# Scores in three bursts of 4, 3 and 3 instead of four, values together, maxima turned at full width, and the transform's sums on GpSimd

## The reference, cut to what matters

```python
q = (x @ wq).reshape(bsz, seq_len, N_HEADS, HEAD_DIM)      # k, v alike, 8 heads; rotary on q and k
scores = jnp.einsum('bqhd,bkhd->bhqk', q, k) / np.float32(np.sqrt(HEAD_DIM)) + mask
attn = jax.nn.softmax(scores.astype(jnp.float32), axis=-1)
out = jnp.einsum('bhqk,bkhd->bqhd', attn, v).reshape(bsz, seq_len, N_HEADS * HEAD_DIM)
return out @ wo
# experts: relu(x W_e + b_e) of the top 2 of 8, averaged; g = silu of it; x = x + s * g
# second layer's kernel: sums over 64 states of v / (g(omega) - Lambda), four of them, 512 roots
cauchy = lambda v: (v[None, :] / denom).sum(-1)
at_roots = c * (k00 - k01 * (1.0 / (1.0 + k11)) * k10)
```

## Time and profile before

| | |
|---|---|
| Time, median of 3 runs | 664.26 us (659.87 to 670.34) |
| Span of the profiled execution | 663.2 us |
| Median less span: what lies around the span | 1.1 us |
| PE busy | 627.2 us, 95% |
| DVE busy | 552.0 us, 83% |
| ACT busy | 287.0 us, 43% |
| POOL busy | 238.2 us, 36% |

### The profile page before, as it was taken

One profiled execution on the slowest core, in us unless ns is written; L12 is line 12 of the kernel. 1 busy time (PEld: TensorE's weight loads), 2 busy tenths in 40 slices (PEclk: granted clock), 3 DMA queues, 4 the chain that ended last, 5 costly groups with the idle time before them and its releaser, 6 DMA issues.

```text
span 663.2 us, 12226 instructions
## 1 busy us (share of the span) xinstructions
PE 627.2 (95%) x3565; PEld 338.9 (51%) x3565; DVE 552.0 (83%) x1788; ACT 287.0 (43%) x535; POOL 238.2 (36%) x364
## 2 busy tenths in 40 slices
PE   8999999998999999999999999999999999789997
PEld 5788784433433334433443344443444343478886
DVE  6698999869978888989888798897789975689994
ACT  4353325434434435444444444443455443444441
POOL 3777641333323212332221322322222115576620
PEclk9999999969989999999999999999999999899999
DMA  7599989889788564675954649667276527768842
GB/s 262 141 336 266 337 239 173 146 164 273 152 268 161 166 139 80 154 132 188 194 105 98 136 109 220 125 173 152 52 167 111 171 72 241 156 145 217 217 104 79
DMA packets 79902, 113.10 MB, mean 171 GB/s; under 512 B 9704, under 2 KB 42664, under 8 KB 79840
## 3 DMA queue, kind: packets, MB, share of 16 engines
q1 hardware_dynamic: 68098, 86.90, 53.5%
q0 software_dynamic: 6704, 18.62, 11.8%
...
## 4 chain that ended last, share of the span: by engine, by line
PE 55%; DVE 25%; DMA 8%; issue 4%; SPq 3%; POOL 2%; ACT 1%; ACTq 0%; DVEq 0%; POOLq 0%
PE bank L1672 13%; DVE bank L1390 12%; PE bank L1023 8%; PE bank L1591 7%; PE bank L2162 6%; PE bank L1644 5%; PE bank L1683 4%; PE bank L2167 4%; DMA w_e<-expert_rows,slots 3%; PE bank L1617 3%; DVE arena L1390 2%; DMA qt<-arena 2%; DMA qt<-turned_parts 2%; DVE m_parts L1403 2%; DVE m_parts L1405 1%
## 5 line engine op out<-in xcount | busy, mean ns | idle before, releaser
L1390 DVE CUSTOM_DVE_ANT_0 bank<-bank,cst 128x384 f32<-128x384 f32 (+3 forms) x512 | 234.9, 521 | 47.6 <-PE bank L1591 44.5
L1514 ACT ACTIVATE arena<-bank 128x512 f32<-128x512 f32 x320 | 170.9, 599 | 180.2 <-PE bank L1617 149.7
L1332 POOL TENSOR_SCALAR_AFFINE_SELECT arena<-arena 128x512 f32<-128x512 f32 x128 | 80.7, 643 | 309.2 <-ACT arena L1514 309.2
L1672 PE MATMUL bank<-w_e,arena 128*128 x312 | 162.2, 626 | 0.0
L1591 PE MATMUL bank<-kt,qt 48*128 48x512 f32 (+1 forms) x496 | 111.0, 338 | 5.6 <-DVE arena L1390 5.0
L1591 PEld LDWEIGHTS bank<-kt,qt 48*128 48x128 f32 x496 | 70.1, 187 | 83.9 <-DVE arena L1390 51.7
L1617 PE MATMUL bank<-qt,kt 50*128 50x512 f32 x256 | 88.2, 452 | 2.4 <-DMA qt<-arena 2.0
L1644 PE MATMUL bank<-arena 128*32 128x512 f32 (+3 forms) x1024 | 84.8, 445 | 0.4 <-ACT arena L1514 0.4
L1672 PEld LDWEIGHTS bank<-w_e,arena 128*128 128x128 f32 x312 | 54.6, 193 | 58.0 <-issue 54.3
L1390 DVE DVE_READ_ACCUMULATOR2_ANT arena<- 128x1 f32 x512 | 71.9, 140 | 0.0
L1683 PE MATMUL bank<-w_proj,arena 128*128 128x512 f32 x128 | 67.6, 636 | 0.0
...
...
## 6 DMA issues: line engine op xcount, KB each, us to landing
...
```

What stands on the lines that cost most here:

```text
L1332: g.affine_select(out=diag, in_=diag, compare_op=ALU.is_ge, fill=0.0, base=0, pattern=[[0, 2], [0, HALF], [1, P]], channel_multiplier=-1). ...
L1390: i = v.tensor_tensor_reduce(out=part, in0=part, in1=const("mask")[:, S - w:], scale=1.0, scalar=LOWEST, op0=ALU.add, op1=ALU.max, accum_o ...
L1514: nc.scalar.activation(pt[:, s, first:second + 1:second - first].rearrange("p c r q -> p c (r q)"), s2_bank(b, h, n).rearrange("p (c x) -> ...
L1672: i = t.matmul(bank[7], xgt[:, m % 2, k * P:(k + 1) * P], w_e[:, ex[m], k, :], start=False, stop=(k == KB - 1))
```

## The change

Scores. The first scores of the following group and the second scores of the group go out in three bursts instead of four: S1(3 to 6) with S2(0 to 3), S1(7 to 9) with S2(4 to 6), and S1(0 to 2) of the group after with S2(7 to 9). All four blocks of values follow each other behind the third burst. `SIZES` has four gaps, with groups of 6, 8, 8 and 6 quarters; names for the first six, the eight and the last six are BACK, EIGHT and FRONT.

Maxima. They are copied unsplit into a wide tile (`maxima_columns`), turned as 128 columns into bank 4 instead of a bank of the first scores, and split after the turning by two operations over 128 x 128 (`maxima_rows`). The turning stands after at most three quarters of the second gap; `normalise` of the group before stands ahead of the split, `pair_rows` behind it.

Queues. SP issues its small transfer of the maxima before the stores of finished expert rows, not behind them. ACT issues its own after exponential 7, or before emptying the bank in groups with four quarters in the second gap.

Sums. Of the six steps of a piece the last four run on POOL (`pool_sums`), at the end of its list for the group, with the sum over 64 states made by halving.

```diff
@@ -45,11 +45,12 @@
 BLOCKS = [(j, t) for j in range(TPB) for t in range(j, TPB)]
 PAIRED = [((0, 0), (0, 1)), ((0, 2), (0, 3)), ((2, 2), (2, 3)), ((1, 1), (3, 3)), ((1, 2), (1, 3))]
 ORDER = [0, 2, 3, 1]
-GAPS = 5
+GAPS = 4
+TURN_AFTER = 3
 PLAN = "x" * 12 + ("ooxoo" + "x" * 9) * 2 + "ooxoo" + "x" * 6
-SIX, EIGHT = (2, 1, 1, 1, 1), (2, 2, 1, 1, 2)
+BACK, EIGHT, FRONT, SIX = (2, 2, 2, 0), (2, 4, 2, 0), (2, 3, 1, 0), (2, 2, 2, 0)
 NONE = (0,) * GAPS
-SIZES = [NONE, (0, 0, 0, 2, 2)] + [SIX, EIGHT] * 12 + [SIX, SIX] + [SIX, EIGHT, (2, 2, 1, 1, 0), NONE]
+SIZES = [NONE, (0, 0, 2, 2)] + [BACK, EIGHT, EIGHT, FRONT] * 6 + [SIX, SIX] + [BACK, EIGHT, FRONT, NONE]
 QUARTERS = [SIZES[KV * b:KV * (b + 1)] for b in range(NB)]
...
@@ -89,10 +90,10 @@
 
     first, last, at = times_of(0), times_of(KB - 1), {}
     for m in range(MT):
-        t = first[m] - 2 + m if m < 2 else max(first[m] - 2, last[m - 2])
-        t += -1 if t % 2 == 0 and (m < 2 or t > last[m - 2]) else t % 2 == 0
-        assert t < first[m]
-        at.setdefault((t // (4 * KV), t // 4 % KV, t % 4 // 2), []).append(m)
+        free = last[m - 2] if m > 1 else GAPS
+        slots = [t for t in range(free, first[m]) if t % GAPS in (1, 2)]
+        t = max([t for t in slots if t < first[m] - 1] or slots)
+        at.setdefault((t // (GAPS * KV), t // GAPS % KV, t % GAPS - 1), []).append(m)
     return at
...
@@ -693,20 +699,35 @@
                 e.wait_ge(dve_steps, st.count())
                 tt(den_r, den_r, den_a, ALU.mult)
                 tt(den_i, den_i, den_a, ALU.mult)
+
+        def pool_sums(e, st, b, h):
+
+            g = nc.gpsimd
+            piece, step = divmod(b * NG + h - 2, 6)
+            if piece not in range(NB) or step < 2:
+                return
+
+            def tt(out, a, b, op):
+                g.tensor_tensor(out, a, b, op).then_inc(pool_steps, st.one())
+                e.wait_ge(pool_steps, st.count())
+
             shape = [P, 4, NS]
             n_r, n_i = (num[:, c].rearrange("p l r n -> p (l r) n") for c in (0, 1))
             d_r, d_i = (d.unsqueeze(1).to_broadcast(shape) for d in (den_r, den_i))
-            for c, x, y, op in ((0, n_r, n_i, ALU.add), (1, n_i, n_r, ALU.subtract)):
-                if h == 2 + 2 * c:
-                    tt(big[0], x, d_r, ALU.mult)
-                    tt(big[1], y, d_i, ALU.mult)
-                if h == 3 + 2 * c:
-                    tt(big[2], big[0], big[1], op)
-                    v.tensor_reduce(part_sum[:, c], big[2], AX.X, ALU.add).then_inc(dve_steps, st.one())
-                    e.wait_ge(dve_steps, st.count())
-            if h == 5:
-                v.tensor_copy(sums[:, :, bass.ds(piece, 1), :], part_sum.unsqueeze(2)).then_inc(dve_steps, st.one())
-                e.wait_ge(dve_steps, st.count())
+            c = step // 2 - 1
+            x, y, op = ((n_r, n_i, ALU.add), (n_i, n_r, ALU.subtract))[c]
+            if step % 2 == 0:
+                e.wait_ge(s4_den, piece + 1)
+                alone(e)
+                tt(big[0], x, d_r, ALU.mult)
+                tt(big[1], y, d_i, ALU.mult)
+            else:
+                tt(big[2], big[0], big[1], op)
+                w = NS // 2
+                while w > 1:
+                    tt(big[2][:, :, 0:w], big[2][:, :, 0:w], big[2][:, :, w:2 * w], ALU.add)
+                    w //= 2
+                g.tensor_tensor(sums[:, c, piece].unsqueeze(2), big[2][:, :, 0:1], big[2][:, :, 1:2], ALU.add).then_inc(s4_sums, 1)
 
         def dve_roots(e, st, step):
...
@@ -1370,14 +1394,18 @@
         QUERIES_OF = ((3,), (3,), (2, 0), (2, 0), (1, 1))
         LOWEST = -3.0e38
 
-        def first_half(n):
-
-            return (n + 1) % 2, n // 2
+        def first_half(b, h, n):
+
+            return (n + (b * NG + h < 2)) % 2, n // 2
+
+        def turned_at(b, h):
+
+            return bank[(0, 1)[h] if b * NG + h < 2 else 4][:, 0:P]
 
         def maxima(e, b, h, n):
 
             v = nc.vector
-            s, kind = first_half(n)
+            s, kind = first_half(b, h, n)
             if n == 0 and due(at := nth_of(1, b, h, 0)):
                 e.wait_ge(b_mx, at)
             e.wait_ge(b_s1, nth_of(NJ, b, h, n + 1))
...
@@ -1392,25 +1420,22 @@
                 at += w
             i.then_inc(b_m, 1)
 
-        def maxima_parts(e, st, b, h):
+        def maxima_columns(e, b, h):
+
+            e.wait_ge(b_m, nth_of(NJ, b, h, NJ))
+            rows = row_max.rearrange("p (s r) t -> p s (r t)", s=2)
+            nc.vector.tensor_copy(m_cols[:, :, 0:2], rows.unsqueeze(2).to_broadcast([P, 2, 2, HALF * TPB])).then_inc(b_mx, 1)
+
+        def maxima_rows(e, st, b, h):
 
             v = nc.vector
-            e.wait_ge(b_m, nth_of(NJ, b, h, NJ))
-            if due(at := nth_of(1, b, h, 0)):
-                e.wait_ge(b_tm, at)
-            e.wait_ge(dve_steps, st.count())
-            rows = row_max.rearrange("p (s r) t -> p s (r t)", s=2)
-            v.tensor_scalar(m_parts[:, :, 0], rows, -1.0, None, ALU.mult).then_inc(dve_steps, st.one())
-            e.wait_ge(dve_steps, st.count())
-            v.scalar_tensor_tensor(out=m_parts[:, :, 1], in0=rows, scalar=-1.0, in1=m_parts[:, :, 0].bitcast(F32),
-                                   op0=ALU.mult, op1=ALU.subtract).then_inc(b_mx, 1)
-
-        def maxima_rows(e, b, h):
-
             e.wait_ge(b_tm, nth_of(1, b, h, 1))
             if due(at := nth_of(32, b, h, 0)):
                 e.wait_ge(b_mr, at)
-            nc.vector.tensor_copy(m_rows, S1_BANK[nth_of(NJ, b, h, NJ + 2) % 3][0:2 * 2 * HALF * TPB, 0:P]).then_inc(b_me, 1)
+            v.tensor_copy(m_high[:, :], turned_at(b, h)).then_inc(dve_steps, st.one())
+            e.wait_ge(dve_steps, st.count())
+            v.scalar_tensor_tensor(out=m_rows[:, :], in0=m_high[:, :].bitcast(F32), scalar=const("less"), in1=turned_at(b, h),
+                                   op0=ALU.mult, op1=ALU.add).then_inc(b_me, 1)
 
         def dve_b(e, st):
             v = nc.vector
...
@@ -1463,25 +1488,27 @@
                     following = next_group(b, h, 1) if b * NG + h + 1 < NB * NG else None
                     after = next_group(b, h, 2) if b * NG + h + 2 < NB * NG else None
                     if following:
-                        for n in (2, 3, 4):
+                        for n in (3, 4, 5, 6):
                             maxima(e, *following, n)
                     done, later = next_group(b, h, -1), h > 0 and following
                     rows_of(*done)
                     if not later:
                         divided(*done)
                     if following:
-                        for n in range(5, NJ):
+                        for n in (7, 8, 9):
                             maxima(e, *following, n)
-                        maxima_parts(e, st, *following)
+                        maxima_columns(e, *following)
+                    if later:
+                        normalise(*done)
+                    if following:
+                        maxima_rows(e, st, *following)
+                    if later and done[1] % 2:
+                        pair_rows(done[0], done[1] // 2)
                     for m in TURNS.get((b, h, 0), ()):
                         expert_x(m)
-                    if following:
-                        maxima_rows(e, *following)
                     if after:
-                        for n in (0, 1):
+                        for n in (0, 1, 2):
                             maxima(e, *after, n)
-                    if later:
-                        divided(*done)
                     if (b, h) == (NB - 1, NG - 1):
                         dve_tap_parts(e)
                         dve_scale(e)
...
@@ -1533,20 +1562,22 @@
 
             def go(b):
                 for h in range(1 if b == 0 else 0, NG):
-                    for n in (0, 1, 2):
+                    following = next_group(b, h, 1) if b * NG + h + 1 < NB * NG else None
+                    for n in (0, 1, 2, 3):
                         exps(e, b, h, n)
                     results(b, h, 0)
-                    for n in (3, 4, 5):
+                    for n in (4, 5, 6):
                         exps(e, b, h, n)
+                    early = len(WORK[b, h, 1]) > TURN_AFTER
+                    if following and early:
+                        maximum_rows(e, *following, 1)
                     results(b, h, 1)
-                    for n in (6, 7):
-                        exps(e, b, h, n)
-                    results(b, h, 2)
-                    if b * NG + h + 1 < NB * NG:
-                        maximum_rows(e, *next_group(b, h, 1), 1)
+                    exps(e, b, h, 7)
+                    if following and not early:
+                        maximum_rows(e, *following, 1)
                     for n in (8, 9):
                         exps(e, b, h, n)
-                    results(b, h, 3, 4)
+                    results(b, h, 2, 3)
 
             for b in range(NB):
                 go(b)
...
@@ -1569,15 +1600,15 @@
```

(35 more changed lines are left out.)

46 lines of the change are left out of this document (28 added, 18 removed).

## The result

The changed kernel takes 688.25 us (median of 4 runs, 685.90 to 690.95). The kernel before, run on the same chip, takes 665.40 (4 runs, 659.87 to 670.34). The ratio is 1.0335, with a 95% interval from 1.0299 to 1.0372: 3.3% slower, some 22 us, and outside the range of the prediction.

What follows compares the result with a forecast made beforehand. PE was taken to set the pace, DVE having little to spare. The order saves 12 us, late DVE adds 1.5 and waits for stacks 14: 3.5 slower than the median 664.3, about 667 us (range 660 to 676).

Steps and rivals of the forecast that it cites:

- new order with its DVE waits: PE's order over groups 2 to 30: some 12 us less, with 1.5 us more for late DVE in groups 2 and 3.
- PE idle for the stacks: PE waits for queries and keys before the third burst: six waits of 2.2 us and one of 0.6, 14 us more.
- The stacks arrive later: Prediction's section on SP's 12 loads of queries and keys: they land after PE needs them behind FRONT groups, 14 us more.
- I take 2.2: Assumed wait in us for stacks in each of six BACK groups, from a span of 1.2 to 3.0, or 3.7.
- The deadline: After FRONT, the BACK group's third burst needs the stacks at T+11.9 us, T being the start of the turning.
- The rule that I cited: 16 partitions reach 4 of 16 ports, 104 GB/s at 1 MiB; by it alone the 12 loads would take 11.3 us.
- The wait in the burst of four: Fourth score pair waits 0.63 us for DVE to read its bank; burst 1.78 us, 18 us over 29 groups.
- The timetable: PE's work by group: BACK 12.7, EIGHT 14.3, FRONT 12.0 us; four groups 53.2 against 54.9 before.
- the transform's sums cost nothing: Four of six sum steps moved from DVE to POOL: hidden in POOL's idle time, no wait of PE ends in them.
- The stacks in time: Rival: the 12 loads find emptier queues and land in time, 653 us; chance 0.18.
- No wait in the burst of four: Rival: that wait is absent or absorbed by the turning's own wait, 18 us less, 649 us; chance 0.10.
- The slower one: Rival: stores ahead of the loads weigh fully, FRONT costs 3.7 and first EIGHT 1.0 us, 682 us; chance 0.16.
- POOL's sums holding DVE up: Rival: GpSimd's sums delay DVE or a select in up to 16 groups, 10 us more, 677 us; chance 0.06.

Runs made afterwards that it cites:

- both kernels without loads: The 12 stack loads in groups of odd h left out of each kernel: changed kernel 653.06 us, kernel before 660.93 us.
- the waits filled: Changed kernel with 14 matmuls on constants into idle bank 7 before the first scores that wait for stacks, in six groups: 678.56 us.
- the experiment with alternating halves: Changed kernel with the 12 stack loads going to lower and upper half of the partitions in turn: 684.34 us.
- the fourth pair apart: Changed kernel with queries loaded in two parts, and the burst of four made three pairs, one quarter, the fourth pair, one quarter: 655.04 us.
- the split loads: Changed kernel with the second group's queries in six later transfers on their own semaphore: 659.92 us; the same on the kernel before: 665.35 us.
- the sums on DVE: Changed kernel with the four sum steps of each piece moved back from POOL to DVE: 688.18 us.

## Why the prediction was wrong

It said 667 us; it is 688.25. The order and its waits for DVE came out nearly as worked out, the price of the waits for the stacks did not. By the forecast's sum against what was measured:

| term | forecast | measured | by |
|---|---|---|---|
| new order with its DVE waits | -10.5 | -7.9 | both kernels without loads |
| PE idle for the stacks | +14 | +20.2 | waits of PE in the trace after |
| clock behind those waits | none | +9.7 | the waits filled |
| sum | +3.5 | +22.0 | 22.85 between the medians |

**The failed step is the price of the waits in "The stacks arrive later": "I take 2.2" for each of six, "14 us" in all.** It was too low twice: the loads were taken as too short, which is 6.2 us, and a wait was charged with its own length alone, so that the clock behind it stood in the sum at nothing, which is 9.7 us.

**The length of the loads.** The deadline was right: PE could begin S1(0) at 269.44, 11.67 after the turning of the FRONT group (forecast T+11.9). The issue came even sooner than forecast, at T+1.80 where no store stands ahead and T+2.24 with one (forecast T+2.43). But the loads took 12.4 to 13.5 us behind FRONT groups, 13.0 in the mean, so that PE waited 2.55 to 3.92, 3.11 in the mean of six. The 2.2 stands for loads of 11.7 us. I took that from 14 cases before and held it fixed, though the change moves the loads against POOL's gathers. Of the excess of 1.3 us, about 1.1 go with the gathers, by the experiment that moved them; the rest stays open.
The rule that I cited, the Trainium skill's "SBUF — State Buffer", section "Door 1: The DMA port swizzle", gave 11.3 us for these loads, and I wrote that the trace agrees. The kernel after does not agree: 13.0, for the same bytes to the same partitions. The measurement decides, and the experiment with alternating halves found no gain by other ports.

**The clock.** The sum charges a wait with its own length. A sign against this stood in the trace of before, outside the stretch of the earlier trace rows, whose clock is 1.00: behind a wait for a transfer of the maxima, of 1.32 us, 3.4 us ran at the lower level. Order of time on PE, then the stretch (window, length, PE busy, granted clock, DMA share, GB/s):

```profile
190.99 0.50 PE L1617 MATMUL bank<-qt,kt 50*128 50x512 f32 x2 [1.32 <-DMA qt<-arena]
```

```profile
191.50:194.90 3.40, 3.40 (x8) 0.50 1.04 351
```

In the kernel after each of the six long waits, and the one of 1.36 us too, was followed by some 3.4 to 7 us at the lower level. Summed from the stretches behind the six long ones, (1 - clock) times length comes to 12.6 us; filling them gave back 9.7.

**What was right.**
- The wait in the burst of four: 1.78 us for the burst, to the hundredth. The hundredth is luck: the fourth pair starts 1.34 us after the burst (forecast 1.45) and then takes 0.44 (forecast 0.33). That the wait costs 18 us over 29 groups was not measured by itself; the fourth pair apart, which buys it back for 0.4 us of new starts and gains 0.2 a group, fits it. The trace shows just 0.33 idle before S1(6), since the ends of matmuls are modelled; read the starts.
- The timetable, mostly: four groups without waits for stacks take 53.30, 52.84, 53.39 and 53.33 (53.2), with one four of 55.49 among them. From the turning of one EIGHT to that of the next it is 14.24 and 14.28 us in two of six pairs (14.3), but 14.9 to 15.0 in the other four, and in three of these the turning waits 0.7 us for DVE, where the timetable had no wait; the other groups make up for it. The -7.9 falls 2.6 us short of the -10.5 in part because the comparison without loads speeds the old order up as well: between the turnings of group 3 and group 30 the old order takes 366.94 us without loads and 372.12 with them. The new order without loads takes 361.33 there.
- That FRONT followed by BACK is the tight place, that EIGHT is not, and that the transform's sums cost nothing. DVE's share fell by 5 points, 3 forecast; POOL's rose by 4, as forecast.

**The rivals.** The stacks in time: refuted by the rows. Its 653 is close to the 653.06 without loads, but in part by luck: leaving the loads out also takes away the 5.4 us that they cost the old order, and with the split loads nearly in time it is 659.92. No wait in the burst of four: refuted. The slower one, the stores ahead of the loads: its time of 682 is nearest to the result, but its mechanism fell; with the stores out of the way the loads were as slow, 12.3 to 13.4 us. POOL's sums holding DVE up: refuted by the sums on DVE.
